# Four heads of 96 channels as three products of 128: the last attention of a four-layer kernel

## The reference, cut to what matters

```python
B, Q, D = 16, 64, 512            # as called here
H, KV, HD = 16, 4, 96            # 16 query heads in 4 groups of 4, 96 channels each
q = (latents @ Wq.T)             # -> (b, KV, G, q_len, HD)
k = (hidden @ Wk.T)              # hidden = concat(context, latents); -> (b, KV, 128, HD)
v = (hidden @ Wv.T)
scores = einsum('bkgqd,bksd->bkgqs', q, k) / sqrt(HD)
attn = softmax(scores)
out = einsum('bkgqs,bksd->bkgqd', attn, v)      # -> (b, q_len, 16 * 96)
x = x + out @ Wo.T
```

## Time and profile before

| | before |
|---|---|
| runs shown, us | 1756.19, 1757.48, 1755.74 (median 1756.19) |
| profiled execution: time, us | 1755.4 |
| its span from first to last instruction, us | 1753.6 |
| mean granted TensorE clock | 0.98 |
| busy: PE / PEld / DVE / ACT / POOL, us | 1637.9 / 1317.7 / 848.9 / 721.2 / 509.9 |
| share of the span | 93% / 75% / 48% / 41% / 29% |
| last attention's part of the span | about 1324.5 to 1753.6 us |

### The profile page before, as it was taken

One profiled execution on the slowest core, in us unless ns is written; L12 is line 12 of the kernel. 1 busy time (PEld: TensorE's weight loads), 2 busy tenths in 40 slices (PEclk: granted clock), 3 DMA queues, 4 the chain that ended last, 5 costly groups with the idle time before them and its releaser, 6 DMA issues. The chain is left out here.

```text
span 1753.6 us, 26179 instructions
## 1 busy us (share of the span) xinstructions
PE 1637.9 (93%) x9762; PEld 1317.7 (75%) x9762; DVE 848.9 (48%) x1757; ACT 721.2 (41%) x2404; POOL 509.9 (29%) x615
## 2 busy tenths in 40 slices
PE   6988898799999999999999987799999998999997
PEld 5877777688888888888888876565456686777775
DVE  3566565454444555544444375767642222343343
ACT  3455444344444544544545542232221123444431
POOL 5657663321222221222222232333210001511122
PEclk9999998999999999999999999899999999999999
DMA  7000001011010101010101000030000003010000
GB/s 226 14 7 7 7 1 37 25 54 37 25 37 25 37 25 37 25 37 25 37 25 37 2 1 19 6 135 1 1 19 1 24 19 93 1 43 25 1 13 36
DMA packets 25855, 53.84 MB, mean 31 GB/s; under 512 B 15088, under 2 KB 16624, under 8 KB 22272
## 3 DMA queue, kind: packets, MB, share of 16 engines
q1 hardware_dynamic: 24048, 51.65, 8.9%
q10 hardware_dynamic: 1616, 0.51, 0.1%
q0 software_dynamic: 64, 0.00, 0.0%
HBM read 50.06 MB, written 2.10 MB: 30 GB/s over the span
## 5 line engine op out<-in xcount | busy, mean ns | idle before, releaser
L1642 ACT ACTIVATE big<-pb 128x128 f32<-128x128 f32 x384 | 106.6, 278 | 313.6 <-PE pb L729 202.2
L1989 POOL TENSOR_TENSOR big<-big 128x512 f32<-128x512 f32 x96 | 100.3, 1044 | 300.1 <-DVE big L1313 299.2
L1693 ACT ACTIVATE big<-pb,big 128x128 f32<-128x128 f32 x384 | 136.1, 367 | 84.7 <-issue 49.2
L793 PE MATMUL pb<-woh,oh 128*128 128x512 f32 (+1 forms) x384 | 165.4, 431 | 5.4 <-DVE wol L1126 2.9
L1308 DVE TENSOR_REDUCE big<-pb 128x4 f32<-128x512 f32 x96 | 66.1, 689 | 185.5 <-PE pb L768 171.8
L1100 DVE TENSOR_TENSOR X<-X,pb 128x512 f32<-128x512 f32 x128 | 87.6, 684 | 135.0 <-PE pb L793 83.6
L793 PE MATMUL pb<-woh,ol 128*128 128x512 f32 (+1 forms) x384 | 151.5, 394 | 0.0
L744 PE MATMUL pb<-wkh,CXh 128*128 128x256 f32 x512 | 149.5, 292 | 1.5 <-DVE big L1298 1.5
L793 PE MATMUL pb<-wol,oh 128*128 128x512 f32 (+1 forms) x384 | 150.3, 391 | 0.0
L744 PE MATMUL pb<-wkl,CXh 128*128 128x256 f32 x512 | 144.3, 282 | 0.0
L744 PE MATMUL pb<-wkh,CXl 128*128 128x256 f32 x512 | 143.6, 281 | 0.0
(11 more groups left out here) (247 smaller groups left out, 3897.6 us busy)
## 6 DMA issues: line engine op xcount, KB each, us to landing
big<-in_w SPq DMA_DIRECT2D x21, 1024.0 KB, 5.0
big<-in_w SPq DMA_DIRECT2D x8, 512.0 KB, 3.6
big<-in_w SPq DMA_DIRECT2D x4, 768.0 KB, 4.1
X<-in_x SPq DMA_DIRECT2D x8, 256.0 KB, 5.3
big<-in_cn SPq DMA_DIRECT2D x8, 256.0 KB, 2.7
CXlf<-in_cT SPq DMA_DIRECT2D x8, 256.0 KB, 5.2
big<-in_wa SPq DMA_DIRECT2D x1, 2048.0 KB, 7.9
big<-in_wb SPq DMA_DIRECT2D x1, 2048.0 KB, 13.5
```

The source lines that it names most:

```text
L793: a = pe.matmul(bank(p), x[0:hd, 512 * k + h * 128:512 * k + h * 128 + 128], y[0:hd, 512 * h:512 * h + 512], start=(n == 0), stop=(n == 11))
L1642: y = a.activation(sq[i % 2], bank(p)[:, j * width:j * width + 128], ACT.Square, accum_out=ss[i % 2][:, first + j:first + j + 1])
L1693: y = a.activation(e_[:, c], bank(p)[:, c], ACT.Exp, bias=m[j % 2][:, k:k + 1], scale=1.0, accum_out=z[j % 2][:, k:k + 1])
L1989: g.tensor_tensor(quarters(e_), quarters(e_), bc(r[j % 2], 128), MUL).then_inc(*on.to(S.pn))
```

## The change

Keys, queries and the output projection of the last attention treat the 4 x 96 = 384 channels of the four heads as three blocks of 128. Block c holds head c's 96 channels in partitions 0 to 95 and the c-th third (32 channels) of the fourth head in partitions 96 to 127. The weights are put in that order on the host (`packed`), and `Wo`'s rows fill 128 partitions instead of 96.

- Products: 36 instead of 48 in each of 4 key blocks and 8 query blocks, 9 instead of 12 in each of 32 projections. They use 128 output channels or rows instead of 96.
- Keys and queries: ScalarE copies partitions 0 to 95 of three tiles instead of four. VectorE then moves partitions 96 to 127 of each tile to the fourth head's place, at partitions 0, 32 and 64, and releases the bank. VectorE waits for ScalarE's copy first (`S.k3`, `S.q3`). Three query tiles use the ring of two banks, as four did.
- Output: `oh3` and `ol3` hold 3 x 128 columns. ScalarE copies the first three heads (96 partitions, 384 columns). VectorE, behind it, copies the three thirds of the fourth head (32x128 each) from PSUM to partitions 96 to 127 of `oh3`, subtracts for the first three heads (96x384), and subtracts for the three thirds.
- `wo3` is split in three column blocks of 128 partitions instead of four of 96, loads are 768 KB instead of 1024 KB, and semaphores of their own (`S.wo3h`, `S.wo3l`, `S.oh3`) replace shared ones.

```diff
     if stage == "l3_kv":
-        return ([(f"k{h}", (1 + h % 2,)) for h in range(4)] if i % 2 == 0
+        return ([(f"k{c}", (1, 2)) for c in range(3)] if i % 2 == 0
                 else [(f"v{b}", (3 + b % 2,)) for b in range(2 * i - 2, 2 * i + 2)])
     if stage == "l3_q":
-        return [(k, (k % 2,)) for k in range(4)] if i % 4 == 0 else []
+        return [(c, (0, 1)) for c in range(3)] if i % 4 == 0 else []
...
-            def project(p, o, hd, k, parts):
+            def project(p, o, size, k, parts):
...
-                for h in range(4):
+                for c in range(size):
                     for x, y in three(*parts):
-                        a = pe.matmul(bank(p), x[0:hd, 512 * k + h * 128:512 * k + h * 128 + 128],
-                                      y[0:hd, 512 * h:512 * h + 512], start=(n == 0), stop=(n == 11))
+                        lo = (size * k + c) * 128
+                        a = pe.matmul(bank(p), x[:, lo:lo + 128], y[:, 512 * c:512 * c + 512], start=(n == 0),
+                                      stop=(n == 3 * size - 1))
...
             def l3_q(i):
...
-                for k in range(4):
+                for k in range(3):
...
-                            a = pe.matmul(bank(p)[0:96, :], y[:, c * 384 + k * 96:c * 384 + k * 96 + 96],
+                            a = pe.matmul(bank(p), y[:, c * 384 + k * 128:c * 384 + k * 128 + 128],
                                           x_tiles(x, c, t, 4), start=(n == 0), stop=(n == 11))
...
 VectorE, keys (l3_kv, even units)
+                    for c in range(3):
+                        p = PSUM["l3_kv", i, f"k{c}"]
+                        on.wait_ge(S.k3, 3 * g + c + 1)
+                        on.wait_ge(p.full, p.n + 1)
+                        if g == 0:
+                            y = v.tensor_copy(k3_rows(0, 3, 4, third(c)), bank(p)[96:128, :])
+                        else:
+                            for s in range(2):
+                                y = v.tensor_copy(k3_rows(4 * g + 2 * s, 3, 2, third(c)),
+                                                  bank(p)[96:128, 256 * s:256 * s + 256]
+                                                  .rearrange("p (t w n) -> p t w n", t=2, w=2))
+                        y.then_inc(p.free, 1)
...
 VectorE, queries (l3_q)
+                if i == 0:
+                    on.wait_ge(f2_done.full, f2_done.n + 1)
+                else:
+                    s = PSUM["l3_a", i - 1, "p"]
+                    on.wait_ge(s.full, s.n + 1)
+                for c in range(3):
+                    p = PSUM["l3_q", i, c]
+                    on.wait_ge(S.q3, 3 * (i // 4) + c + 1)
+                    on.wait_ge(p.full, p.n + 1)
+                    v.tensor_scalar(Q3[third(c)].rearrange("p (b h q) -> p b h q", h=4, q=64)[:, :, 3, :],
+                                    bank(p)[96:128, :].rearrange("p (b q) -> p b q", b=8), 96 ** -0.5, None,
+                                    MUL).then_inc(p.free, 1)
...
 VectorE, output (l3_v)
-                out_low(PSUM["l3_v", i, "p"], 64 + i, 96, oh3, ol3)
+                p, k = PSUM["l3_v", i, "p"], 384 * (i % 2)
+                hi, lo = [x[:, k:k + 384].rearrange("p (h b q) -> p h b q", h=3, b=2) for x in (oh3, ol3)]
+                o = bank(p).rearrange("p (b h q) -> p h b q", b=2, h=4)
+                on.wait_ge(S.oh3, i + 1)
+                for c in range(3):
+                    on.mark(v.tensor_copy(hi[96:128, c], o[third(c), 3]))
+                v.tensor_tensor(lo[0:96], o[0:96, 0:3], hi[0:96].bitcast(F32), SUB)
+                on.wait_ge(S.dve, on.n)
+                for c in range(3):
+                    y = v.tensor_tensor(lo[96:128, c], o[third(c), 3], hi[96:128, c].bitcast(F32), SUB)
+                y.then_inc(p.free, 1)
...
 ScalarE
-                a.copy(high[0:hd, k:k + 512].rearrange("p (h b q) -> p b h q", h=4, b=2),
-                       bank(p)[0:hd].rearrange("p (b h q) -> p b h q", b=2, h=4)).then_inc(S.oh, 1)
+                a.copy(oh3[0:96, k:k + 384].rearrange("p (h b q) -> p b h q", h=3, b=2),
+                       bank(p)[0:96].rearrange("p (b h q) -> p b h q", b=2, h=4)[:, 0:3]).then_inc(S.oh3, 1)
...
+            def third(c):
+                return slice(32 * c, 32 * c + 32)
...
+    packed = np.concatenate([np.r_[96 * k:96 * k + 96, 288 + 32 * k:320 + 32 * k] for k in range(3)])
```

More of the change, by code:

```diff
@@ L957, in l3_kv @@
                     on.wait_ge(S.w3kl, 3)
-                    for h in range(4):
-                        p = PSUM["l3_kv", i, f"k{h}"]
+                    for k in range(3):
+                        p = PSUM["l3_kv", i, f"k{k}"]
                         on.wait_ge(p.free, p.n)
@@ L1000, in l3_a @@
                 h, t = divmod(i, NT)
[L1001 to L1007, removed]
+                p = PSUM["l3_a", i, "p"]
+                for c in (1, 2):
+                    q, k3 = PSUM["l3_q", i // 4 * 4, c], PSUM["l3_kv", 6, f"k{c}"]
+                    on.wait_ge(q.free, q.n + 1)
+                    on.wait_ge(k3.free, k3.n + 1)
                 on.wait_ge(p.free, p.n)
@@ L1028, in l3_c @@
             def l3_c(i):
-                on.wait_ge(S.wol, 32 + 4 * (i // NT) + 4)
-                project(PSUM["l3_c", i, "p"], PSUM["l3_v", i, "p"], 96, i % 2, (oh3, ol3, woh3, wol3))
+                on.wait_ge(S.wo3l, 3 * (i // NT) + 3)
+                project(PSUM["l3_c", i, "p"], PSUM["l3_v", i, "p"], 3, i % 2, (oh3, ol3, woh3, wol3))
             def f3_mm(t):
@@ L1328, in l1_v @@
             def l1_v(i):
-                out_low(PSUM["l1_v", i, "p"], i, 128, oh, ol)
+                p, k = PSUM["l1_v", i, "p"], 512 * (i % 2)
+                hi, lo = [x[:, k:k + 512].rearrange("p (h b q) -> p b h q", h=4, b=2) for x in (oh, ol)]
+                on.wait_ge(S.oh, i + 1)
+                v.tensor_tensor(lo, bank(p).rearrange("p (b h q) -> p b h q", b=2, h=4), hi.bitcast(F32),
+                                SUB).then_inc(p.free, 1)
             def l1_d(i):
@@ L1474, in l3_c @@
                 if t == NT - 1 and h < 3:
-                    low_parts(wol3, woh3, wo3[h + 1], 96, 4, S.woh, S.wol, 9 + h)
+                    low_parts(wol3, woh3, wo3[h + 1], 3, S.wo3h, S.wo3l, h + 1)
                 if 8 <= i < 16 and i % 2 == 0:
@@ L1523, in high_parts @@
                     c = slice(512 * j, 512 * j + 512)
[L1524 removed]
+                    a.copy(hi[:, c], raw[:, c]).then_inc(high, 1)
             def begin(_):
@@ L1720, in l1_v @@
                     on.wait_ge(l0_done.full, l0_done.n + 1)
-                out_high(PSUM["l1_v", i, "p"], i, 128, oh)
+                p, k = PSUM["l1_v", i, "p"], 512 * (i % 2)
+                if i >= 2:
+                    w = PSUM["l1_d", i - 2, "p"]
+                    on.wait_ge(w.full, w.n + 1)
+                on.wait_ge(p.full, p.n + 1)
+                a.copy(oh[:, k:k + 512].rearrange("p (h b q) -> p b h q", h=4, b=2),
+                       bank(p).rearrange("p (b h q) -> p b h q", b=2, h=4)).then_inc(S.oh, 1)
             def copy_bf16(p, dst):
@@ L1811, in l3_kv @@
                     on.wait_ge(read.full, read.n + 1)
-                for h in range(4):
+                for h in range(3):
                     p = PSUM["l3_kv", i, f"k{h}"]
@@ L1820, in l3_kv @@
                                        .rearrange("p (t w n) -> p t w n", t=2, w=2))
-                    y.then_inc(p.free, 1)
+                    y.then_inc(S.k3, 1)
             def l3_main(_):
-                high_parts(woh3, wo3[0], 96, 4, D.wo3, 16, S.woh)
+                high_parts(woh3, wo3[0], 3, D.wo3, 16, S.wo3h)
             def l3_q(i):
@@ L1850, in l3_v @@
             def l3_v(i):
-                out_high(PSUM["l3_v", i, "p"], 64 + i, 96, oh3)
+                p, k = PSUM["l3_v", i, "p"], 384 * (i % 2)
+                if i >= 2:
+                    w = PSUM["l3_c", i - 2, "p"]
+                    on.wait_ge(w.full, w.n + 1)
+                on.wait_ge(p.full, p.n + 1)
+                a.copy(oh3[0:96, k:k + 384].rearrange("p (h b q) -> p h b q", h=3, b=2),
+                       bank(p)[0:96].rearrange("p (b h q) -> p h b q", b=2, h=4)[:, 0:3]).then_inc(S.oh3, 1)
             def l3_c(i):
@@ L1857, in l3_c @@
                     on.wait_ge(w.full, w.n + 1)
-                    high_parts(woh3, wo3[h + 1], 96, 4, D.wo3, 16 * (h + 2), S.woh)
+                    high_parts(woh3, wo3[h + 1], 3, D.wo3, 16 * (h + 2), S.wo3h)
                 if 8 <= i < 16 and i % 2 == 0:
@@ L2171, in l3_main @@
                 load(b3h, d["b3"], D.f3)
-                on.wait_ge(S.wol, 36)
-                load(wo3[1], d["w3"][1][:, 1536:3584], D.wo3)
+                on.wait_ge(S.wo3l, 3)
+                load(wo3[1], d["w3"][1][:, 1536:3072], D.wo3)
             def l3_q(i):
```

109 lines of the change are left out of this document (52 added, 57 removed).

## The result

| | before, beside it | changed |
|---|---|---|
| median of four runs, us | 1755.97 (1750.16 to 1757.48) | 1768.84 (1767.55 to 1771.09) |
| ratio, 95% interval | | 1.0081 [1.0056, 1.0106] |
| profiled execution: time / span, us | 1755.4 / 1753.6 | 1767.55 / 1765.8 |
| mean granted TensorE clock | 0.980 | 0.966 |

The forecast was 1743.3 with a range of 1730 to 1758. The sign is wrong and the time lies outside the range.

A forecast was written before the change was run, and what follows sets the result against it. The prediction took the key stage as TensorE bound and the attention loop as latency bound. Keys -11.1, start -4.9, rounds -6.4, banks +3.1, `w3l` +1.5 and tail +4.9 gave -12.9 us: 1743.3 us, range 1730 to 1758.

The forecast's parts named there:

- keys and start: Key stage: four blocks 2.78 us shorter each, -11.1 us; first two query blocks, at the pipeline's start, -4.9 us.
- terms for keys and queries: Key stage -11.1 us, pipeline start -4.9 us, and 2.78 us less for the query block in each of six rounds.
- the loop is bound by latency: Attention loop: the chain projection, weighing, `oh`, `ol` sets the step; it changes by 1.49 - 0.69 = +0.80 us.
- end to end: VectorE's seven operations in `l3_v` run without overlap, 2.30 us, taking 0.26 us for a small one.
- Rival (a): VectorE overlaps the seven operations in `l3_v`: chain 1.89 us, step +0.39, total 1731 us; chance 0.20.
- Rival (b): Small moves between partitions in `l3_v` cost 0.35 us each: chain 2.84, step +1.34, total 1761 us; chance 0.10.
- the 0.31 us: Time of a small VectorE operation from which rival (b) decides, where the forecast's sum is zero.
- (c) The clock: Idle TensorE in loop steps lowers its clock: up to 2.6 us a stretch, one in each of 8 rounds 1764; chance 0.07.
- the tail: Last linear layer: longer `l3_v` delays `CXl` and its products one for one, seven steps at +0.80, last projection -0.69: +4.9 us.
- stretches under 1.00 in the loop: Sign that would show the prediction wrong: the clock row has stretches under 1.00 in the attention loop.
- `w3l`, `w3fl` and the banks: Query blocks: third tile waits for its bank in three steps, +3.1 us; `l3_v` late behind `w3l` and `w3fl`, +1.5 us.
- terms for the output part: Output projection's terms: steps +0.80 us each, projections behind query blocks -0.69 each, tail +4.9, lateness behind `w3l` +1.5.

The follow-up runs named there:

- qk_only: Changed kernel with the output projection and l3_v put back as before, keys and queries of 128 kept; 1722.93 us, ratio 0.9813 to the kernel before.
- no_shift: Changed kernel, but in units 2 to 23 the six small VectorE operations stay in partitions 0 to 31 (output not the reference's); 1745.99 us, ratio 0.9931.
- fill_loop: Changed kernel plus six unused TensorE products before the wait for `ol` in units 0 to 23's steps without a query block; 1759.41 us, ratio 1.0018.
- fill_both: Changed kernel with the loop's unused products and six more ahead of each of the last layer's eight product groups; 1752.47 us, ratio 0.9978.
- o_only: Changed kernel with keys and queries put back as before, the output projection of 128 and its seven VectorE operations kept; 1791.52 us, ratio 1.0208.

## Why the prediction was wrong

**Right: keys and start.** -10.8 and -5.3 against -11.1 and -4.9, and qk_only as a whole gives -33 where the prediction's terms for keys and queries add up to -11.1 - 4.9 - 6 x 2.78 = -32.7. A product of 128 costs what one of 96 does. A step with a query block took 12.72 us where nothing stood in its way, exactly 16.19 - 0.69 - 2.78.

**Right: the loop is bound by latency,** and the seven operations lie end to end. 2.42 against 2.30 us for VectorE's part, because a small operation is 0.28 to 0.30 and not 0.26; over 18 steps 2 to 3 us. Rival (a), with overlap, did not happen here; no_shift shows that it would have in one partition group. Rival (b)'s 0.35 was too dear. But the row that decided for "end to end" was read wrongly, and that it pointed the right way was luck: the second operation of the earlier trace rows adds to what the first wrote and the kernel makes it wait for it, so it could not have overlapped. The two 128-column "subtractions" of the earlier trace rows are an addition and a multiplication (L1204, L1360). And the 0.31 us at which rival (b) is said to decide should be 0.33 by the prediction's own two points, 0.26 with -12.9 and 0.35 with +4.9.

**Wrong: "(c) The clock ... Chance 0.07".** This is the step that failed. The prediction wrote down that a step leaves TensorE idle 1.7 of 6.1 us, and it does (1.73 of 6.30). It then priced the loop and the tail at full clock: the sum has no term for the clock. For it stood one stretch with 4.48 of 6 busy at 1.00. Two rows at 0.50 to 0.56 stood on the other side, and no row showed the clock under a repeated idle of this size; the range left rival (c)'s 1764 out. One of the prediction's own signs of being wrong, stretches under 1.00 in the loop, came true. What the runs show:

- five of 18 steps 1.57 us longer, 7.9 us;
- the six steps with a query block 86.3 us instead of 6 x 12.72 = 76.3, of which 3.4 is the bank wait: 6.6 us (fill_loop takes 11.3 of these 14.5 back);
- 8.7 us in the tail (against fill_both).

Together 23.2 us. So -12.9, +23.2 for the clock, +4.1 in the rounds and +1.4 in the tail (both below), and -3.6 ahead of the key stage make the measured +12.2. Without the clock and that -3.6 the changed kernel would be some 7 us under the one before (-12.9 + 4.1 + 1.4), an estimate; the nearest run, fill_both, which still has some of its tail at the lower clock, is 3.6 us under it. So the clock turned the sign, and the forecast was still too good without it. The one-per-round price of rival (c), 1764, came near by luck: it took 2.6 us for a stretch and eight of them, and the six rounds alone had nine steps that it lengthened, by 1.6 us each, with more in the tail. The Trainium skill, TensorE: Matmul & The Clock Gate, section "A second HAM failure mode: psum-queue depth-cycling", tells of frequent short idles between groups of products that make the clock swing; the trace agrees, with 0.78 and 1.00 in neighbouring steps.

**Off in size: `w3l`, `w3fl` and the banks.** The bank waits are 3.4 us, forecast 3.1 (4.5 in fill_loop, where little of the clock mixes in). What is late behind the splits is 3.5 us in five steps of fill_loop, forecast 1.5. With the 2 us of the small operations that is the +4.1. The late steps are those where VectorE has `w3l` (three, forecast 0.5 each) or `w3fl` ahead of the seven operations. The two with `w3l` alone are 0.6 late and the two with `w3fl` alone 0.35. The largest (7.70 us there, 7.73 in the changed kernel) has both. There, and in the two with `w3fl` alone, this subtraction took 1.03 to 1.16 us instead of 0.68; in the changed kernel's largest it ran beside GpSimd's work (an ordinary one is shown last):

```profile
1536.81 1.90 DVE L1131 TENSOR_TENSOR w3l<-big,w3h 128x512 fp32r<-128x512 f32 x3
...
1538.87 1.04 POOL L2034 TENSOR_TENSOR big<-big 128x512 f32<-128x512 f32 x1 [14.80 <-DVE big L1318]
...
1539.43 1.03 DVE L1522 TENSOR_TENSOR w3fl<-big,w3fh 128x512 fp32r<-128x512 f32 x1
...
1573.01 0.68 DVE L1522 TENSOR_TENSOR w3fl<-big,w3fh 128x512 fp32r<-128x512 f32 x1
```

The traces hold a clue to it. From 1440 us on, the changed kernel has 22 subtractions for `w3l`, `wol` and `w3fl`; the five of them that took longer than 0.70 us (0.94 to 1.52) are the five that ran while GpSimd was at work. In the kernel before it is three of 29. The shorter projection lets the sum into X start sooner, and that puts three of four `w3fl` beside GpSimd's product, where it was one of four. No run took GpSimd's work away, so the cause is not shown.

**Off in size: the tail.** Forecast +4.9, measured +6.3 at near full clock (fill_both, 83.3) and +15.0 with the clock. The mechanism, `CXl` behind a longer `ol`, was right: eight waits, 18.3 us for 8.0.

**Left unseen in the sum itself.** The prediction's own terms for the output part, 18 x 0.80 - 6 x 0.69 + 4.9 + 1.5 = +16.7 us, say that this half loses. Added to a gain of 32.7 the loss was hidden. Measured alone it is +35.4. The two halves don't add up to the whole (-33.2 + 35.4 = +2.2, measured +12.9). Most of the other 10.7 us is again the clock, by an estimate. Against the kernel before, the six rounds are 16.0 us shorter in qk_only, 23.3 longer in o_only and 16.8 longer in the changed kernel: 9.5 of the 10.7 lie there. They ran at 0.93 in the changed kernel and at 0.97 in o_only, whose three slow steps cost 5.8 us, with no query-block step at the lower clock, against the 14.5 above. Why the combination falls more often was not tried.

## What to carry to other kernels

Price each half of a change alone: a loss that is visible in the working is easy to overlook beside a larger gain. Where a loop waits on latency, fewer products gain nothing by themselves, they lengthen TensorE's idle time, and then the clock itself can go down, as it did here; products that need only what is ready early should go first. Here seven operations, six of them small and moving between partition groups, took 2.42 us where one large one took 0.70; such moves belong on an engine that has time to spare, or nowhere.

## What the runs showed that was not expected

- Useless products made the changed kernel faster: 48 fillers in the tail and 108 in the loop gained 16 us.
- The granted clock stayed at 1.00 for 18 steps with 1.31 us idle in 6.52 and fell in 5 of 18 with 1.73 in 6.30, in 9 of 18 with 2.29 in 7.52. What decides in which of like steps it falls stays open.
- VectorE's small operations: 0.30 to 0.32 us apart when they start in changing partition groups, 0.21 to 0.22 when they start in one, with 32 partitions as with 96.
